# Three attentions computed by key tiles instead of query tiles

## What is computed

```python
q = (q_in @ Wq.T + bq).reshape(B, T, H, HD) * HD ** (-0.5)
k = (kv_in @ Wk.T + bk).reshape(B, S, H, HD)
v = (kv_in @ Wv.T + bv).reshape(B, S, H, HD)
att = jax.nn.softmax(jnp.einsum('bthd,bshd->bhts', q, k), axis=-1)
o = jnp.einsum('bhts,bshd->bthd', att, v).reshape(B, T, D)
return o @ out_w.T + out_b
```

## Time and profile before

| | |
|---|---|
| median of 3 runs | 3323.68 us (3322.3 to 3328.46) |
| the profiled execution, its own time | 3329.74 us |
| its span in the trace | 3327.9 us |
| mean granted clock of TensorE | 0.949 of full speed |
| busy: TensorE | 2957.0 us, 89% of the span |
| busy: VectorE | 2030.3 us, 61% |
| busy: ScalarE | 1465.1 us, 44% |
| busy: GpSimd | 944.3 us, 28% |

### The profile page before, as it was taken

How to read it: one execution, slowest core, us unless ns; L and a number is a source line. 1 busy time by engine, 2 the same in 40 slices (tenths; PEclk the granted TensorE clock), 3 DMA queues, 4 the chain that set the end, 5 groups by cost and what they waited for, 6 DMA issues and landing times. The chain is left out here.

```text
span 3327.9 us, 47565 instructions
## 1 busy us (share of the span) xinstructions
PE 2957.0 (89%) x15718; PEld 2057.7 (62%) x15718; DVE 2030.3 (61%) x4335; ACT 1465.1 (44%) x3160; POOL 944.3 (28%) x994
## 2 busy tenths in 40 slices
PE   5978789998589968699998888989999899998898
PEld 3522287776557644244445665568777687776787
DVE  8989746776421126599996345652777537776444
ACT  1000035665135426466664345533666436664322
POOL 2057664671134330566661000000000000001210
PEclk9999999999689979799999899989999999999899
DMA  3047765331559953544441453226431154311322
GB/s 99 13 142 206 199 154 133 63 74 41 166 179 341 340 172 141 195 137 140 137 126 57 162 143 77 50 68 189 87 71 25 25 189 91 79 25 39 104 82 82
DMA packets 222607, 402.70 MB, mean 121 GB/s; under 512 B 44222, under 2 KB 140626, under 8 KB 218526
## 3 DMA queue, kind: packets, MB, share of 16 engines
q1 hardware_dynamic: 170866, 262.09, 27.7%
q0 software_dynamic: 49744, 134.92, 14.6%
q10 hardware_dynamic: 1756, 2.64, 0.3%
HBM read 315.84 MB, written 87.71 MB: 121 GB/s over the span
## 5 line engine op out<-in xcount | busy, mean ns | idle before, releaser
L904 ACT ACTIVATE at_p<-at_pb,at_max 125x1250 f32<-125x1250 f32 (+4 forms) x320 | 383.8, 1199 | 301.9 <-DVE at_unused L975 273.5
L790 PE MATMUL at_pb<-ident,at_p 125*125 125x125 f32 x2880 | 433.0, 281 | 20.0 <-ACT at_p L904 17.0
L790 PEld LDWEIGHTS at_pb<-ident,at_p 125*125 125x125 f32 x2880 | 390.2, 190 | 83.0 <-ACT at_p L904 22.3
L807 PE MATMUL at_pb<-at_pt,at_v 125*64 125x250 f32 x2880 | 355.7, 384 | 5.2 <-DVE s_t L1008 3.0
L968 DVE TENSOR_REDUCE at_wide<-at_pb 125x1 f32<-125x1024 f32 x240 | 293.6, 1224 | 21.0 <-PE at_pb L773 2.7
L890 ACT ACTIVATE at_pt<-at_pb 125x500 f32<-125x500 f32 (+1 forms) x448 | 232.8, 520 | 96.3 <-PE at_pb L790 91.9
L807 PEld LDWEIGHTS at_pb<-at_pt,at_v 125*64 125x64 f32 x2880 | 188.6, 137 | 104.0 <-issue 14.4
L750 PE MATMUL at_pb<-at_s,at_shared 128*128 128x500 f32 (+1 forms) x1152 | 229.3, 361 | 23.4 <-ACT at_shared L852 23.4
L986 DVE COPY at_pt<-at_pb 125x500 f32<-125x500 f32 (+1 forms) x416 | 232.3, 582 | 21.6 <-PE at_pb L790 21.6
L975 DVE TENSOR_SCALAR_CACHE_REDUCE at_unused<-at_pb,at_wide 125x226 bf16<-125x226 f32 x240 | 107.8, 449 | 204.7 <-PE at_pb L773 201.7
L750 PEld LDWEIGHTS at_pb<-at_s,at_shared 128*128 128x128 f32 x1152 | 196.0, 194 | 56.4 <-ACT at_shared L852 24.2
(11 more groups left out here) (336 smaller groups left out, 5695.1 us busy)
## 6 DMA issues: line engine op xcount, KB each, us to landing
w_ring<-in_L_ffn_w SPq DMA_DIRECT2D x128, 512.0 KB, 11.5
at_shared<-k_parts SPq DMA_DIRECT2D x64, 312.5 KB
ml_w<-in_mlp_w SPq DMA_DIRECT2D x64, 256.0 KB
k_parts<-at_shared SPq DMA_DIRECT2D x64, 250.0 KB, 2.9
q_parts<-at_shared SPq DMA_DIRECT2D x64, 250.0 KB, 2.8
h_edges<-em_both SPq DMA_DIRECT2D x11, 1024.0 KB, 4.1
g_h<-h_edges SPq DMA_DIRECT2D x11, 1024.0 KB, 5.7
at_shared<-q_parts SPq DMA_DIRECT2D x32, 312.5 KB
```

Source lines behind the costliest of these rows:

```text
L790: ins = pe.transpose(pturn[0:TN, g % 2, TN * (t % 4):TN * (t % 4) + TN], p[:, u % 2, TN * t:TN * t + TN], c.ident[0:TN, 0:TN])
L807: ins = pe.matmul(pout[side:side + 64, 0:2 * TN], v[:, t, 2 * j + h, :], p_t[:, q % 2, t, :], start=(t < 2), stop=(t >= keys[u] - 2))
L904: act.activation(p[:, t % 2, 0:w], score[t % 2][0:TN, 0:w], ACT.Exp, bias=neg_max[:, t:t + 1], accum_out=total[:, t:t + 1]).then_inc(exp_d ...
```

## The change

A new function, `attention_by_key`, takes over the three attentions without a mask; the causal one stays as it was. The projections go in the order q, k, v, and so `load_first` is given q's first half. The loop has 16 passes, each of one head and 625 queries (half of them), and a pass goes over the 10 key tiles: 160 steps. In a step TensorE forms transposed scores, `[125 keys, 2 x 313 queries]`: two products with the high part of k as stationary operand (128 rows, against q's high and low part), and two with the low part (65 rows, against q's high part; row 64 of the one side is ones and of the other side the negated maximum, so the maximum is taken off by the product). ScalarE's exponent goes from PSUM to SBUF for all 626 columns at once, and the result goes into the product with v as it is: two products of 313 columns, one for each half of the 625 queries, with 64 output columns each. The maxima come ahead of all this, by products of their own: 15 for each pass (five sets of 125 queries, taken with a step of five, by three cuts of about 417 keys), reduced by VectorE and collected with one minimum, and SyncE moves the 625 numbers into row 64 by a DMA. The maxima of a pass run 13 steps ahead of it; those of the first pass and more stand between v's projections. The row sums are formed from the exponents: GpSimd adds five of the ten tiles, in layer 0 three, and VectorE the others (in the spatial and cross attention four additions on each engine, in layer 0 two and six), and four products with ones as stationary operand add the partitions; VectorE takes the reciprocal of the result in PSUM and multiplies twice. The products for maxima and for sums take turns in two PSUM banks (4 and 5). In layer 0 the 160 indirect writes are 56 first and the others between GpSimd's additions. The core of it, the projections left out:

```diff
+QUARTERS = ((0, 312), (622, 314))
+MAX_CUTS = ((0, 418), (418, 834), (834, N))
...
+        RINGS, DEEP = 4, 8
...
+        for P in range(PASSES):
+            for k in range(15):
+                pieces_at[NT * P - LEAD + 10 * k // 15].append((P, k // 3, k % 3))
+        sums_at = {NT * P + NT + 2: P for P in range(PASSES)}
...
+        by_pool = [(0, 1), (5,)] if send is not None else [(0, 2), (4,), (6,), (8,)]
...
+                    if x in (begin[1] + 1, begin[3] + 1):
+
+                        for r in range(RINGS):
+                            sp.wait_ge(stored[r], stores_by(begin[ci], r))
+                        load_pair(sp, 0, kind, first_in)
...
+                for P in range(PASSES):
+                    j, h, half = P // 4, P // 2 % 2, P % 2
+                    sp.wait_ge(max_ready, P + 1)
+                    sp.dma_start(qb[j % 2][h][MAXROW, 625 * half:625 * half + 625].bitcast(F32).rearrange("o (p i) -> o p i", p=TN),
+                                 neg[:, P, :].bitcast(F32)).then_inc(row_in, 16)
...
+                            load_pair(sp, j + 1, "qk", kq_in[(j + 1) % 2])
...
+                def max_pieces(s):
+                    for P, i, n in pieces_at[s]:
...
+                        k = slot_of[P, i, n]
...
+                        if k >= 2:
+                            pe.wait_ge(freed, k - 1)
+                        a, b = MAX_CUTS[n]
+                        pe.matmul(bank[0:TN, 4 + k % 2, 0:b - a], qa[j % 2][h][:, 625 * half + i:625 * half + 625:5], ka[j % 2][h][:, a:b],
+                                  start=True, stop=True).then_inc(filled, 1)
...
+                    if kind == "v":
+                        if x == first_v:
+
+                            pe.wait_ge(first_in, 16 * LOADS)
+                            pe.wait_ge(low, first_v)
+                        for s in steps_after(x - first_v):
+                            max_pieces(s)
+
+                def scores(s):
...
+                    if t == 0:
+                        pe.wait_ge(row_in, 16 * (P + 1))
...
+                    if s >= 2:
+
+                        pe.wait_ge(exp_done, s - 1)
...
+                    for x in range(2):
+                        pe.matmul(at(x), ka[j % 2][h][:, keys], qa[j % 2][h][:, slice(*chunk(half, x))], start=True, stop=False)
+                    for x in range(2):
+                        ins = pe.matmul(at(x), kb[j % 2][h][0:65, keys], qb[j % 2][h][0:65, slice(*chunk(half, x))],
+                                        start=False, stop=True)
+                    ins.then_inc(scored, 1)
+
+                def values(s):
...
+                    for x in range(2):
+                        ins = pe.matmul(bank[64 * x:64 * x + 64, 6 + P % 2, 0:wide(half)], v[:, t, 2 * j + h, :],
+                                        p[:, s % DEEP, x, 0:wide(half)], start=(t == 0), stop=(t == NT - 1))
+                    ins.then_inc(pv_done, 1)
+
+                def sums(P):
+                    k, w = sum_slot[P], wide(P % 2)
+                    pe.wait_ge(freed, k - 1)
...
+                    for g in range(2):
+                        for x in range(2):
+                            ins = pe.matmul(bank[64 * x:64 * x + 64, 4 + k % 2, 0:w], ones[:, :], acc[:, P % 2, g, x, 0:w],
+                                            start=(g == 0), stop=(g == 1))
+                    ins.then_inc(filled, 1)
+
+                for s in range(STEPS + 4):
+                    if s < STEPS:
+                        scores(s)
+                    max_pieces(s)
+                    if 2 <= s < STEPS + 2:
+                        values(s - 2)
+                    if s in sums_at:
+                        sums(sums_at[s])
...
+                    act.activation(p[:, s % DEEP, :, 0:w], bank[0:TN, b:b + 2, 0:w], ACT.Exp).then_inc(exp_done, 1)
...
+                def scale(P):
...
+                    dve.reciprocal(inverse[:, P % 2, 0:w], bank[:, 4 + k % 2, 0:w]).then_inc(freed, 1)
+                    dve.wait_ge(freed, k + 1)
+                    dve.wait_ge(pv_done, NT * (P + 1))
+                    for x in range(2):
+                        dve.tensor_tensor(out_t[64 * h:64 * h + 64, j, slice(*chunk(half, x))],
+                                          bank[64 * x:64 * x + 64, 6 + P % 2, 0:w], inverse[64 * x:64 * x + 64, P % 2, 0:w],
+                                          ALU.mult).then_inc(scaled, 1)
+
+                for s in range(STEPS + 4):
+                    max_pieces(s)
+                    if 2 <= s < STEPS + 2:
+                        add(s - 2)
+                    if s in sums_at:
+                        scale(sums_at[s])
...
-            attention(nc, c, s_t, s_t, s_t, *halves, None, None, scratch, send=(table1, rows1, slots1),
+            attention_by_key(nc, c, s_t, s_t, s_t, *halves, None, None, scratch, send=(table1, rows1, slots1),
```

More of the change, by code:

```diff
@@ L2435, in program @@
                 normalize(nc, c, x_sb, x_out=x1, keep=keep0, targets=[(s_t, col("ln1_g"), col("ln1_b"))],
-                          next_in=load_first(c, halves[1]))
+                          next_in=load_first(c, halves[0]))
             late0, late1 = ExitStack(), ExitStack()
@@ L2490, in program @@
                           early=all_w(a["tp_w"]), columns=(bcol(a["tv_bcol"]), all_b(a["tp_b"])), after=lambda wo: out_features(
-                              nc, c, t_t, wo, load_first(c, whalf(sw, 1), (bcol(sbr, 0), bcol(sbr, 1)), spatial), residual_d=t_d))
-                attention(nc, c, s_t, s_t, s_t, whalf(sw, 0), whalf(sw, 1), whalf(sw, 2), bcol(sbr, 0), bcol(sbr, 1), scratch,
+                              nc, c, t_t, wo, load_first(c, whalf(sw, 0), (bcol(sbr, 0), bcol(sbr, 1)), spatial), residual_d=t_d))
+                attention_by_key(nc, c, s_t, s_t, s_t, whalf(sw, 0), whalf(sw, 1), whalf(sw, 2), bcol(sbr, 0), bcol(sbr, 1), scratch,
                           pick=spatial, early=all_w(a["sp_out_w"]), ahead=True, columns=(bcol(sbr, 2), all_b(a["sp_out_b"])),
                           after=lambda wo: out_features(nc, c, s_t, wo, load_first(
-                              c, zero(whalf(cw, 1)), (zerob(bcol(cbr, 0)), zerob(bcol(cbr, 1))))))
+                              c, zero(whalf(cw, 0)), (zerob(bcol(cbr, 0)), zerob(bcol(cbr, 1))))))
                 def out1(wo):
@@ L2499, in out1 @@
                     out_tokens(nc, c, s_t, wo, late[1], x4, keep1, bias_d=a["cross_out_b"])
-                attention(nc, c, s_t, t_t, s_t, zero(whalf(cw, 0)), zero(whalf(cw, 1)), zero(whalf(cw, 2)),
+                attention_by_key(nc, c, s_t, t_t, s_t, zero(whalf(cw, 0)), zero(whalf(cw, 1)), zero(whalf(cw, 2)),
                           zerob(bcol(cbr, 0)), zerob(bcol(cbr, 1)), scratch, early=lambda e: kview(a["cross_out_w"]), after=out1,
```

355 lines of the change are left out of this document (added).

## The result

The changed kernel takes 3527.25 us (median of 4 runs, 3514.23 to 3530.16) against 3326.07 (4 runs) for the one before: a ratio of 1.060, with an interval of 1.056 to 1.063, 201 us more. The forecast was 3483, with a range of 3350 to 3600. The profiled execution is the shortest of the four, 3514.2 us, so the traces show 184.5 of the 201 us.

The account below looks back on a forecast made before the run. TensorE, with no slack in the three attention loops, was taken as the bound. Terms (a) to (h) sum to +53 us an attention, three times 159 us, on the median of 3323.7: 3483 us, range 3350 to 3600.

Parts of the forecast that it names:

- (a): TensorE's own work in the loop: transposes go, products for maxima, sums and changes of width come; +6 us an attention.
- (b): VectorE's reciprocal of the sums holds a PSUM bank that TensorE's maxima need: 14 waits of 1.85, +26 us an attention.
- (c): Maxima between v's projections: the third piece waits for the first one's bank after six items, +7 us an attention.
- (d): First loads: k comes second and TensorE waits for its six loads after v's first item, +3 us (0 to 6).
- (e): Row of maxima by DMA: queues behind the next pair's loads three times, just in time, +1 us (0 to 6).
- (f): Loop's ramp and tail: the inverse's way through DRAM, GpSimd's scalings and weight copies go, -2 us (-6 to +2).
- (g): Clock: the loops get a lower granted clock, as the causal loop did at 0.94; +10 us an attention (0 to 19).
- (h): VectorE's and GpSimd's work in the loop is covered unless their additions block each other, +2 us an attention (0 to 24).
- second rival: VectorE becomes the loop's bound, its additions blocked beside GpSimd's: 20 us more an attention, 3543 up to 3640; chance 0.13.
- first rival: VectorE's reciprocal is as cheap as any pass over PSUM: 18 us an attention, 3378 us (3335 to 3430); chance 0.20.
- The third: Rival: TensorE's changes to half-width value products and back cost nothing, not 0.35 us a step; 3315 or 3285; chance 0.10.

Follow-up runs that it names:

- after: The changed kernel itself, with the new loop in three attentions, against the kernel before: 3527.25 us, ratio 1.060.
- the last but one kernel: Against the combined-edits kernel with VectorE's list reordered: in layer 0, 58 table writes ahead instead of 80, four GpSimd additions a pass instead of five; 3309.26 us.

## Why the prediction was right or wrong

The mechanism held: TensorE's own work doesn't shrink, and waits that the old loop didn't have come on top. That the total came as near as it did is partly luck, since one term was far too low and several others too high. By its terms, for the cross attention (58.4 us more, 53 forecast):

| term | forecast | measured |
|---|---|---|
| (a) TensorE's own work | +6 | +22: 160 x 1.45, 220 maxima x 0.25 and 16 x 1.05 are 303.8 in the loop, 286.4 before; 20 more maxima stand in v |
| (b) reciprocal | +26 | +21: 14 waits, 1.5 us of pitch each |
| (c) maxima in v | +7 | +4.4 |
| (d) first loads | +3 | +1: a wait of 2.7, and 1.5 less in the other projections |
| (e) row of maxima | +1 | +3.0, once |
| (f) ramp and tail | -2 | about -5, what is left of the loop |
| (g) clock | +10 | +10, an estimate: (1 - 0.98) x 337 + (1 - 0.92) x 45 |
| (h) VectorE, GpSimd | +2 | 0; 5 to 6 in layer 0 |

The measured ones sum to 56; 2 us aren't placed. Layer 0 took 13 us more than the cross attention, which the forecast, one number for all three, didn't have: its wait for k's first loads was 6.0 us, its sums came late (h), and its loop was granted 0.96 and not 0.98.

- The step that was mis-sized most is in (a): "I take 0, as for the loads that are seen". A load with a step of five is not like those; at 0.30 us it no longer fits beside a product of 0.19, and 240 of them made (a) 16 us an attention too low, 48 in all. The upper bound of 46 an attention had it in. That is more than the traces' whole excess: the three attentions took 188 us more where 159 were forecast, 29 over, since (b), (c), (d) and (f) were, in the cross attention, each too high by 2 to 5 us. Of the 44 us between 3483 and the median of 3527 a further 17 are that the profiled execution was the shortest of the four.
- (b): the slope from two rows of 1 and 10 columns gave 2.4 us for 314, and it is 2.12. A half with 157 columns took 1.13, so 6.3 ns a column. The estimate from the repeat count of 8, the Trainium skill, VectorE: DVE Perf Modes, section "First, the fixed hardware budget", was 2.6, and the measurement is lower. The prediction says that the step from 1 to 10 columns agrees with it, but 7.2 ns a column isn't the 8.3 that 2.6 us for 314 come to. The cause was only half right: the prediction said that the bank is freed late, and the run with the copy shows that a free bank without a free VectorE is worse than nothing.
- (c), (d), (e): each wait is where the prediction had it and 0.7, 2.3 to 6.0 and 3.0 to 3.3 us long. (e) came at the second pass only, and there the row wasn't "just in time".
- (g): the size is right, as far as the estimate goes. The later expectation that the lower clock goes with the wait ahead of it isn't borne out: two runs took waits away, and their traces have it at other waits.
- (h): in layer 0 the sums came 0.4 us late in 13 passes, between 5 and 6 us in all. VectorE's last addition ahead of them was held up beside one of GpSimd's, as the timelines of VectorE, GpSimd and TensorE show for one of these passes:

```profile
650.58 0.80 DVE L1482 TENSOR_TENSOR ak_acc<-ak_acc,ak_p 125x624 f32<-125x624 f32 x1
...
652.79 1.69 DVE L1482 TENSOR_TENSOR ak_acc<-ak_acc,ak_p 125x624 f32<-125x624 f32 x1
...
652.30 1.52 POOL L1248 TENSOR_TENSOR ak_acc<-ak_p 125x628 f32<-125x628 f32 x1 [5.02 <-ACT ak_p L1411]
...
654.59 1.27 PE L1349 MATMUL ak_pb<-ak_acc,ak_ones 125*64 125x312 f32 x8 [0.22 <-issue]
```

The addition takes 0.80 us where GpSimd is at none; here it takes 1.69 and ends 0.66 us after GpSimd's, and the sums start 0.11 us behind it. The rule of the Trainium skill in SBUF — State Buffer, section "Who interferes with whom", agrees. The second rival was thus a real mechanism with a small price.

The first rival, a cheap reciprocal, fell with 2.12 us. The third, free changes of width, fell with the runs that grouped the values: 0.31 us for a way there and back where nothing else waits, and 0.27 in the run with values between the maxima, against 0.35 forecast. That a change of tiling mode drains TensorE is what the Trainium skill states in TensorEngine Tiling (Array Packing), section "Key Properties"; the traces give the price of the change, and no run here shows that it is a drain.

## What to carry to other kernels

Price an operand's access pattern by a row of that pattern, and give a load that no row shows a value inside its bounds, not at the end: the one term taken at its lower bound made the largest error. Where an engine's long instruction sits between two others' exchange of buffers, freeing the buffer isn't enough; look at what stands behind it in that engine's list, and cut or move the instruction. Removing work from a full engine pays only when the way back into its stream is counted: here the transposes went and the changes of width came. With grouped values and a spread reciprocal the new spatial loop was about as long as the old one (294 us against 296); it was shorter with neighbouring operands and the edits beside them (279), and again with VectorE's list in another order and more additions on GpSimd (272).

## What was not expected of the hardware

- A stationary operand of 125 columns read with a step of five took 303 ns to load, with neighbouring columns 188 to 193.
- The granted clock after waits of about the same length differed (a pass is taken here from one set of products with ones to the next). Behind the 42 waits of 1.2 us of after, 30 passes were granted 0.98 to 1.00 and 12 were granted 0.86 to 0.92. Behind the 42 waits of 1.7 us of the run with the copy, 5 passes, all in layer 0, were at 1.00, and in the cross attention all 14 were at 0.84 to 0.86. In the 272 us of the last but one kernel's spatial loop, with four waits, none over 1.5 us, the clock was 1.00. What decides it is open.
- With waits taken away in v's projections and the 14 of each loop left, the traced execution had a higher clock in v's projections (1.00, where after had 0.89 to 0.92) and a lower one in the loops (0.95 to 0.96, where after had 0.96 to 0.98). One execution of each doesn't show that the one brings the other.
